# Odd steps of a state-space scan: rows brought by a repeating DMA and copied to PSUM by ScalarE instead of a spreading matmul

## The reference, cut to what matters

```python
xr, gate = jnp.split(x @ W_in.T, 2, axis=-1)
...
xc = silu(conv(xr))                        # 4 taps, over tokens
xn = (xc - mu) / jnp.sqrt(var + 1e-05) * ln_g + ln_b
Bm, Cm, dt = jnp.split(xn @ W_xproj.T, 3, axis=-1)
...
def step(h, inputs):
    ad, bd, xt, ct = inputs
    h = jnp.clip(h * ad[:, :, None] + bd[:, :, None] * xt[:, None, :], -10.0, 10.0)
    yt = jnp.einsum('bd,bdh->bh', ct, h)
    return (h, yt)
_, ys = jax.lax.scan(step, h0, ...)        # 1024 steps, one behind the other
y = ys + D * xn
return y * jax.nn.silu(gate) @ W_out.T
```

## Time and profile before

| what | value |
|---|---|
| median of 3 runs | 6216.15 us (6211.86 to 6225.62) |
| profiled execution, own time | 6190.74 us |
| its span | 6188.9 us |
| mean granted PE clock | 0.972 of full speed |
| attention phase | 0 to about 3142 us |
| first to last step of the scan | 3323 to 6097 us |
| the tail behind it | 6097 to 6189 us |

### The profile page before, as it was taken

The page is one execution under the profiler, slowest core; times in us unless marked ns, Lnnn a source line. Parts: engine busy times, 40 slices in busy tenths (PEclk is TensorE's granted clock), DMA queues, the critical chain, the costliest instruction groups (busy, mean ns, idle before and its releaser), DMA issues. The chain is left out here.

```text
span 6188.9 us, 73250 instructions
## 1 busy us (share of the span) xinstructions
PE 5830.7 (94%) x24000; PEld 2703.2 (44%) x24000; DVE 4474.3 (72%) x5676; ACT 2407.5 (39%) x4698; POOL 3217.6 (52%) x2625
## 2 busy tenths in 40 slices
PE   7999999999999999999986879999999999999998
PEld 3444444444444444444443424444443444444343
DVE  4656656556556566565546998999999898999983
ACT  2444444445444454444453424243332423334111
POOL 1876767677667776775743323425243443524213
PEclk7999999999999999999988889999999999999999
DMA  2332323333232332323213343534444443544433
GB/s 86 89 91 69 99 73 94 91 88 89 76 96 77 98 93 69 106 60 96 82 67 109 87 113 103 147 96 131 110 116 126 121 133 89 150 96 128 115 91 115
DMA packets 411565, 613.30 MB, mean 99 GB/s; under 512 B 58768, under 2 KB 189968, under 8 KB 410672
## 3 DMA queue, kind: packets, MB, share of 16 engines
q1 hardware_dynamic: 374320, 558.24, 32.4%
q10 hardware_dynamic: 36864, 50.38, 3.2%
HBM read 305.31 MB, written 201.38 MB: 82 GB/s over the span
## 5 line engine op out<-in xcount | busy, mean ns | idle before, releaser
L1126 POOL TENSOR_TENSOR acc<-acc,prob 128x512 f32<-128x512 f32 x1536 | 1906.4, 1277 | 837.3 <-PE bank L815 570.8
L1055 DVE TENSOR_REDUCE mx<-bank 128x1 f32<-128x512 f32 x2048 | 1307.4, 684 | 535.9 <-PE bank L785 529.6
L2091 DVE SCALAR_TENSOR_TENSOR g<-xps,bd,g 128x1024 f32<-128x1024 f32 x1024 | 1313.2, 1282 | 143.8 <-PE xps L1806 68.1
L1806 PE MATMUL xps<-sx,spread 128*128 128x512 f32 x2048 | 910.4, 529 | 140.6 <-DVE g L2091 126.0
L948 ACT ACTIVATE prob<-misc 128x512 f32<-128x512 f32 x1277 | 713.5, 599 | 739.0 <-PE misc L802 653.6
L785 PE MATMUL bank<-khat,qhat 96*128 96x512 f32 x2048 | 939.1, 519 | 5.9 <-DVE mx L1055 0.9
L2097 DVE TENSOR_SCALAR g<-g,lim 128x1024 f32<-128x1024 f32 x1024 | 892.7, 872 | 34.8
L1806 PEld LDWEIGHTS xps<-sx,spread 128*128 128x128 f32 x2048 | 359.0, 195 | 693.8 <-issue 368.0
L802 PE MATMUL misc<-qhat,khat 98*128 98x512 f32 x1443 | 602.6, 460 | 17.8 <-ACT prob L948 11.7
L785 PEld LDWEIGHTS bank<-khat,qhat 96*128 96x128 f32 x2048 | 373.8, 192 | 532.5 <-issue 381.4
L1820 PE MATMUL yps<-g,cexp 128*32 128x512 f32 x4096 | 585.4, 630 | 0.1
(11 more groups left out here) (221 smaller groups left out, 7189.6 us busy)
## 6 DMA issues: line engine op xcount, KB each, us to landing
sx<-scratch_xhl SPq DMA_DIRECT2D x512, 128.0 KB, 4.9
scratch_dx<-dx SPq DMA_DIRECT2D x64, 512.0 KB, 3.2
scratch_xhl<-xhi SPq DMA_DIRECT2D x64, 512.0 KB, 4.9
scratch_xhl<-xn SPq DMA_DIRECT2D x64, 512.0 KB, 5.1
scratch_y<-ysb SPq DMA_DIRECT2D x512, 64.0 KB
dx_t<-scratch_dx SPq DMA_DIRECT2D x59, 512.0 KB, 6.1
y_t<-scratch_y SPq DMA_DIRECT2D x59, 512.0 KB, 3.9
xt_n<-in_x SPq DMA_DIRECT2D x112, 256.0 KB, 3.0
```

Source lines behind the costliest of these rows:

```text
L1055: dve.tensor_reduce(self.mx2[:, h * TT + qt, c:c + 1], bank[m][:, 0:QC], AX.X, ALU.max).then_inc(sem[f"dve_m{m}"], 1)
L1126: pool.tensor_tensor(self.acc[:, a, h, :], self.acc[:, a, h, :], self.prob[:, (n % 2) * GH + h, :], ALU.add).then_inc(sem["pool_acc"], 1)
L1806: mm = pe.matmul(self.xps[t % 2][:, half * BANK:(half + 1) * BANK], self.spread[:, 2 * part + half, :], self.sx[:, n % 2, wd, :], start=Tr ...
L2091: dve.scalar_tensor_tensor(self.g[:, t % 4, :], self.xps[t % 2][:, :], self.bd[:, i % 2, tl:tl + 1], self.g[:, (t - 1) % 4, :], ALU.mult, ...
```

## The change

Even steps are as before. For odd steps:

- the normalised rows of odd tokens are stored from `xn` to a new DRAM tensor `scratch_xrow` after `a2` (`sxr`, two semaphores, 64 partitions of a tile each time); `lo` waits for that store, since it overwrites `xn`. The stores `shi` and `slo` take even tokens only, and `scratch_xhl` is half as large.
- SP loads one row of all 8 batches per odd step, each batch repeated 16 times by a step of zero in the source, into a ring of four buffers of 128 x 1024 in SBUF (`lr`, 512 KB on the SBUF side).
- ACT copies the buffer into the PSUM pair (`xa`), waiting for `q` of step `t - 2` and for the load. A buffer is loaded again when its copy is done, for the step 8 later.
- the matmul pair of odd steps goes, and a unit's four `sx` loads are half as large.
- `q` waits for `g(t-1)` first, then for the copy or the matmul; `x` waits for `q(t-2)` first.
- for room in SBUF, `y_t` and `dx_t` share their memory with constants that are used before them, and the constants' loads of the scan share one semaphore, for which each engine waits when it comes to the scan.

The core of the diff (left out: the merged waits on `ld_const` in the other places):

```diff
@@ -1130,6 +1130,7 @@
 
+ROWS = 4
 LAST_ROOMS = 3
...
@@ -1267,11 +1268,12 @@
                         put("POOL", 1.27, ("a2", i, hb, bb, half), (("a1", i, hb, bb, half),), [("pool_x", 1)], port=True)
+                    put("SP", 0.55, ("sxr", i, hb, bb), (("a2", i, hb, bb, 1),) + ((("sxr", i, hb, bb - 2),) if bb > 1 else was("sxr", *old, HB - 2 + bb)), [(f"st_xr{bb % 2}", 16)], lands=4.0)
                     for half in range(2):
...
                     for half in range(2):
-                        put("POOL", 1.27, ("lo", i, hb, bb, half), (("hi", i, hb, bb), ("sq", i, hb, bb), ("a3", i, hb, bb, half)),
+                        put("POOL", 1.27, ("lo", i, hb, bb, half), (("hi", i, hb, bb), ("sq", i, hb, bb), ("a3", i, hb, bb, half), ("sxr", i, hb, bb)),
                             [("pool_lo", 1)], port=True)
...
@@ -1376,19 +1378,32 @@
             put(n * UNIT - 12.0, "SP", 2.2, ("lu", n), (rows if n * UNIT % TOK == 0 else ()) + (
-                (("x", (n - 1) * UNIT - 1),) if n > 1 else (("rest",),)), [(f"ld_sx{n % 2}", 64)], lands=4.0)
+                (("x", (n - 1) * UNIT - 2),) if n > 1 else (("rest",),)), [(f"ld_sx{n % 2}", 64)], lands=4.0)
+
+        def row(t):
+            i = t // TOK
+            put(t - 7.0, "SP", 0.6, ("lr", t), tuple(("sxr", i, hb, bb) for hb in range(2) for bb in range(HB)) + (
+                (("xa", t - 2 * ROWS),) if t > 2 * ROWS else ()), [(f"ld_xb{t // 2 % ROWS}", 16)], lands=4.0)
 
...
             put(t - 2.0, "PE", 0.45, ("x", t), (("lu", t // UNIT),) + ((("q", t - 2),) if t > 1 else ()), [("pe_xps", 1)])
+
+        def copy_of(t):
+            put(t - 2.0, "ACT", 1.05, ("xa", t), (("lr", t),) + ((("q", t - 2),) if t > 1 else ()), [("act_xps", 1)])
+
         for n in range(2):
             load(n)
-        x_of(0), x_of(1)
+        for t in range(1, 2 * ROWS, 2):
+            row(t)
+        x_of(0), copy_of(1), row(1 + 2 * ROWS)
         for t in range(last):
             i, tl = divmod(t, TOK)
-            put(t, "DVE", 1.3, ("q", t), (("x", t),) + ((("g", t - 1),) if t else (("g0",),)) + ((("d3", i),) if tl == 0 else ()) + (
+            put(t, "DVE", 1.3, ("q", t), (("xa", t) if t % 2 else ("x", t),) + ((("g", t - 1),) if t else (("g0",),)) + ((("d3", i),) if tl == 0 else ()) + (
                 (("out", (t - 4) // 2 * 2),) if t > 3 else ()), [("dve_q", 1)], step=t)
             if t + 2 < last:
-                x_of(t + 2)
+                (copy_of if t % 2 else x_of)(t + 2)
+            if t % 2 and t + 2 + 2 * ROWS < last:
+                row(t + 2 + 2 * ROWS)
             put(t, "DVE", 0.82, ("g", t), (("q", t),), [("dve_g", 1)], port=True)
...
@@ -1449,7 +1464,9 @@
         self.wx = sb("wx", [P, CT, NX])
-        self.wxdt = sb("wxdt", [NST, DIN])
+        early = sb("early", [P, 2 * DIN])
+        y_t, dx_t = early[:, 0:DIN], early[:, DIN:2 * DIN]
+        self.wxdt = early[0:NST, 0:DIN]
         self.wdt = sb("wdt", [NST, NST])
...
@@ -1457,9 +1474,9 @@
         self.mask = sb("mask", [P, 8, 32])
-        self.ones_at = sb("ones_at", [P, 4 * P])
-        self.tmp = sb("tmp", [P, CT, NX])
-        self.ones = sb("ones", [P, P])
+        self.ones_at = early[:, DIN:DIN + 4 * P]
+        self.tmp = early[:, DIN + 4 * P:DIN + 4 * P + CT * NX].rearrange("p (t k) -> p t k", t=CT)
+        self.ones = early[:, DIN + 4 * P + CT * NX:DIN + 5 * P + CT * NX]
         self.gw = sb("gw", [P, NX])
...
@@ -1490,13 +1507,12 @@
 
-        self.sx = sb("sx", [P, 2, UNIT // 2, BANK], F32R)
+        self.sx = sb("sx", [P, 2, UNIT // 4, BANK], F32R)
+        self.xb = sb("xb", [P, ROWS, DIN])
 
...
         self.ysb = sb("ysb", [P, 2, BANK])
-        y_t = sb("y_t", [P, DIN])
-        dx_t = sb("dx_t", [P, DIN])
         sg = sb("sg", [P, DIN])
...
@@ -1598,23 +1614,39 @@
                 w.wait_ge(sem["act_hi"], plan.after("act_hi", ("hi", i, hb, bb)))
-                sp.dma_start(d["xhl"][0, hb * HB + bb, i * TOK:(i + 1) * TOK, :].bitcast(F32),
-                             self.xhi[:, bb % 2, :].bitcast(F32)).then_inc(sem[f"st_xhi{bb % 2}"], 16)
+                sp.dma_start(d["xhl"][0, hb * HB + bb, i * TOK // 2:(i + 1) * TOK // 2, :].bitcast(F32),
+                             self.xhi[0:P:2, bb % 2, :].bitcast(F32)).then_inc(sem[f"st_xhi{bb % 2}"], 16)
             elif kind == "slo":
...
                 w.wait_ge(sem["pool_lo"], plan.after("pool_lo", ("lo", i, hb, bb, 1)))
-                sp.dma_start(d["xhl"][1, hb * HB + bb, i * TOK:(i + 1) * TOK, :].bitcast(F32), self.xn[:, bb, :]).then_inc(
-                    sem[f"st_xlo{bb}"], 16)
+                sp.dma_start(d["xhl"][1, hb * HB + bb, i * TOK // 2:(i + 1) * TOK // 2, :].bitcast(F32),
+                             self.xn[0:P:2, bb, :]).then_inc(sem[f"st_xlo{bb}"], 16)
+            elif kind == "sxr":
+                i, hb, bb = at
+                w.wait_ge(sem["pool_x"], plan.after("pool_x", ("a2", i, hb, bb, 1)))
+                w.wait_ge(sem.get(f"st_xr{bb % 2}"), plan.before(f"st_xr{bb % 2}", p))
+                sp.dma_start(d["xrow"][hb * HB + bb, i * TOK // 2:(i + 1) * TOK // 2, :], self.xn[1:P:2, bb, :]).then_inc(
+                    sem[f"st_xr{bb % 2}"], 16)
+            elif kind == "lr":
+                t, = at
+                i, k = t // TOK, t // 2 % ROWS
+                for hb in range(2):
+                    for bb in range(HB):
+                        w.wait_ge(sem[f"st_xr{bb % 2}"], plan.after(f"st_xr{bb % 2}", ("sxr", i, hb, bb)))
+                if t > 2 * ROWS:
+                    w.wait_ge(sem["act_xps"], plan.after("act_xps", ("xa", t - 2 * ROWS)))
+                sp.dma_start(self.xb[:, k, :], d["xrow"][:, t // 2, :].unsqueeze(1).broadcast_to([B, NST, DIN])).then_inc(
+                    sem[f"ld_xb{k}"], 16)
             elif kind == "lu":
                 n, = at
-                i, s, t0, wd = n * UNIT // TOK, n % 2, n * UNIT, UNIT // 2
+                i, s, t0, wd = n * UNIT // TOK, n % 2, n * UNIT // 2, UNIT // 4
 
...
                 if n > 1:
-                    w.wait_ge(sem["pe_xps"], plan.after("pe_xps", ("x", (n - 1) * UNIT - 1)))
+                    w.wait_ge(sem["pe_xps"], plan.after("pe_xps", ("x", (n - 1) * UNIT - 2)))
                 else:
...
@@ -1796,11 +1828,11 @@
                 n, r = divmod(t, UNIT)
-                part, wd = divmod(r, UNIT // 2)
+                part, wd = divmod(r // 2, UNIT // 4)
+                if t > 1:
+                    w.wait_ge(sem["dve_q"], plan.after("dve_q", ("q", t - 2)))
                 w.wait_ge(sem["dve_set"], plan.after("dve_set", ("rest",)))
                 w.wait_ge(sem[f"ld_sx{n % 2}"], plan.after(f"ld_sx{n % 2}", ("lu", n)))
-                if t > 1:
-                    w.wait_ge(sem["dve_q"], plan.after("dve_q", ("q", t - 2)))
                 for half in range(2):
...
@@ -1992,6 +2023,13 @@
                                bias=self.state_cols[:, 0:1]).then_inc(sem[f"act_m{m}"], 1)
+            elif kind == "xa":
+                t, = at
+                k = t // 2 % ROWS
+                if t > 1:
+                    w.wait_ge(sem["dve_q"], plan.after("dve_q", ("q", t - 2)))
+                w.wait_ge(sem[f"ld_xb{k}"], plan.after(f"ld_xb{k}", ("lr", t)))
+                act.activation(self.xps[t % 2][:, :], self.xb[:, k, :], ACT.Copy).then_inc(sem["act_xps"], 1)
             elif kind == "ysb":
...
@@ -2081,11 +2118,14 @@
                 i, tl = divmod(t, TOK)
-                w.wait_ge(sem["dve_set"], plan.after("dve_set", ("g0",)))
-                w.wait_ge(sem["pe_xps"], plan.after("pe_xps", ("x", t)))
-                w.wait_ge(sem["dve_par"], plan.after("dve_par", ("d3", i)))
                 if t:
                     w.wait_ge(sem["dve_g"], plan.after("dve_g", ("g", t - 1)))
+                if t % 2:
+                    w.wait_ge(sem["act_xps"], plan.after("act_xps", ("xa", t)))
+                else:
+                    w.wait_ge(sem["pe_xps"], plan.after("pe_xps", ("x", t)))
+                w.wait_ge(sem["dve_set"], plan.after("dve_set", ("g0",)))
+                w.wait_ge(sem["dve_par"], plan.after("dve_par", ("d3", i)))
                 if t > 3:
...
@@ -2366,7 +2407,7 @@
     for name, shape, dt in (("rows", (B, 3, HID), F32), ("xs", (B, S, HID), F32), ("x2", (B, S, HID), F32), ("x2T", (HID, B, S), F32),
-                            ("dx", (B, S, DIN), F32), ("xhl", (2, B, S, DIN), F32R),
+                            ("dx", (B, S, DIN), F32), ("xhl", (2, B, S // 2, DIN), F32R), ("xrow", (B, S // 2, DIN), F32),
                             ("y", (B, S, DIN), F32)):
```

More of the change, by code:

```diff
@@ L1523, in __init__ @@
         self.sem = self.plan.sems
-        for name in ("win", "const", "late", "wx", "cols", "sc", "spread", "wxdt"):
+        for name in ("win", "const", "late"):
             name = f"ld_{name}"
@@ L1569, in sync @@
         sp.dma_start(self.mask[:, :, :], d["mask"].rearrange("p (a m) -> p a m", a=8)).then_inc(sem["ld_const"], 16)
```

(24 more changed lines are left out.)

## The result

The changed kernel takes 6456.0 us (6451.5 to 6459.3), the one before 6214.0 us beside it: a ratio of 1.039 (1.037 to 1.041), so it is 3.9% slower.

What follows compares the result with a forecast made beforehand. DVE and PE bound the scan before; eight full DMA engines would after. Middle, first and last parts add 250, 10 and 45 us, +305 on 6216: 6521 us. Own range 6380 to 6660; 8-in-10 range 6070 to 6900.

Steps and rivals of the forecast that it cites:

- Part 5: DMA engines in the scan: row loads fill eight of sixteen, 13.8 us each per unit, becoming the new bound: +305 us.
- the prediction's own test: Lone row loads: the prediction is wrong if they show share 1.0 instead of 0.5, or 0.5 lasting under 2.8 us.
- the prediction's terms: Busiest engines' other work per middle unit: 7.14 us each after removals, plus scratch_y stores, 11.5 engine-us over four engines.
- Part 1: PE in the scan: 512 matmul pairs go, 341 us less PE work in the middle; 101 us of DVE's waits won.
- I count 75: DVE's waits for PE: 75 us counted as won in the middle scan, plus 26 in the last, together 101.
- Part 2: Wait order of `q` in the scan: asking for `g(t-1)` first saves 0.037 us per step, 34 us taken.
- Part 3: 512 ACT copies from SBUF to PSUM at odd steps: 1.05 us each, costing nothing on the path.
- Part 4: SP issues 512 row loads and 64 stores, about 0.4 us each; POOL's wait and the constants' semaphore are also covered.
- Rival A: Row loads run on all sixteen engines, DVE is the bound and 135 us are won: 6081 us; chance 0.21.
- B: Row loads on eight engines at the clean store rate, 22 engine-us per row: about 6185 us; chance 0.12.
- C: Row loads on eight engines with interfering writes, at `khat`'s rate: 4.15 us per row, 27.7 per middle unit; chance 0.21.
- D: ACT's copy late or SP held: 0.3 us at every second odd step, 77 us; chance 0.06.

Runs made afterwards that it cites:

- the spread stores: Changed kernel with scratch_y laid out so its stores have 32 outermost entries and use sixteen DMA engines, row loads unchanged: 6350.4 us, 1.025 of the kernel before.
- sixteen engines: Changed kernel with each odd row stored twice in DRAM, so row loads have sixteen outermost entries, each repeated eight times: 6183.0 us, 0.9979 of the kernel before.
- 16-channel run: Changed kernel whose row loads bring only 16 of 1024 channels, all issues and copies kept: 6123.1 us, 0.989 of the kernel before.
- the ACT queue: Changed kernel with row loads issued by ACT on its own DMA queue instead of SP's: 6648.1 us, 1.073 of the kernel before.
- the half version: Changed kernel where, at odd steps, PE builds channels 0 to 511; a sixteen-engine row load and ACT bring the rest: 6211.7 us, 1.003 of the kernel before.

## Why the prediction was right, and where it was not

Forecast 6521 us, 305 more; measured 6456, 242 more (261 in the profiled spans), inside the forecast's own range of 6380 to 6660.

Part 5, the bound, held, and so did its count: the row loads on eight engines are what costs. The lone row load shows 0.48 where the prediction's own test asked for 0.5. Its price, in engine-us (microseconds of one DMA engine), from a 6 us window around one:

```profile
3525.00:3531.00 6.00, 3.17 (x14) 1.08 (x14) 5.86 (x6) 2.49 (x5) 3.48 (x3) 1.00 0.31 94
```

0.31 x 6 x 16 = 29.8 engine-us, 3.7 us on each of eight; 3.44 was taken from the `affine` load of the earlier trace rows. In bulk: 0.62 x 24.3 x 16 = 241 per unit, less the other work by the prediction's terms, 16 x 7.14 + 11.5 = 126, leaves 28.9 per row, 3.6 us on each engine. By this sum the four busiest carry 10.0 + 4 x 3.6 = 24.4 us of a unit of 2334 / 96 = 24.3, and the other four of the eight 21.5.

So the row was a little too cheap (13.8 for 14.4 us per unit). But the sum now asks for engines without a gap, and the trace has gaps. The longest, in the middle part:

```profile
3944.10:3950.60 6.50, 6.25 (x40) 4.06 (x39) 5.45 (x9) 1.90 (x3) 2.84 (x3) 1.00 0.00 0
```

By the packet records no packet is in flight for 87 of the 2334 us, so no engine can be busy for more than 96%, which is the filling that the prediction took from PE. (It is PE's in the middle part; in the last one has 98%.) Fewer than eight packets are in flight for 21% of the time, so the eight are never all busy for more than 79%. For 10% of the time there are more than sixteen: packet times then overlap on an engine, and engine-us add up to more than busy time. The prices of the sum are therefore too high where the load is heavy, and the 24.8 forecast for 24.3 owes something to errors that cancel. The engines are the bound in the sense that unloading them gives the time back, not in the sense that they are full. That late loads delay the copies, and so the next row loads, would explain the gaps; it was not followed up. By stage: +250, +10 and +45 us forecast, +206, +16 and +37 measured. That the four engines of `scratch_y` are among the eight was an assumption; the 106 us of the spread stores speak for it, and nothing in the traces shows engine numbers. The rule of the Trainium skill that the prediction weighed ("DMA: Bandwidth & Descriptors", "Why a DMA increments its semaphore by 16 and not by 1"), the largest k up to 16 that divides the slowest dimension, fits all three cases: 0.48 with eight entries, 0.26 with four, and with sixteen a share of 0.72, which alone says only more than eight, with sixteen packets in flight.

What failed is where the wait would show. The prediction had ACT's copies and `q` at odd steps wait for the ring. They did so for 9.0 and 15.8 us. (The landing time of the row loads, which it wanted far above 5 us, no view of after gives; with sixteen engines it is 6.1.) It had costed only the row load's own consumer, and passed over the other loads in the same engines: `x2T_t` has one buffer and no lead, so it is the first to suffer, and PE's written order carries the delay to the even steps. The total came out near all the same because it was added up from the load of the engines, and not from who waits; that the two errors of that sum point in opposite directions helped. PE's busy share was forecast at 75% and is 85%: busy time does not fall with the number of matmuls. 769 fewer in the middle part took away 45 us, not 341 (103 us in the 16-channel run, where the granted clock is as before). `xps` halved (682.5 to 341.9 us), while other groups became longer. `yps` rose from 429.7 to 484.9, though one of its matmuls takes 613 ns where it took 620, and to 506.0 in the 16-channel run, so the clock is not the reason there: spans of matmuls overlap, and a group's busy time holds what no neighbour covers. The matmuls that wait for `x2T_t` did take longer each, 681 for 603 ns (372.0 to 423.3 us), at a granted clock of 0.93 instead of 0.99.

Part 1 was sized too high, which no one sees in after, but the 16-channel run does: parts 1 and 2 without the bytes are worth 70 us, not 135. By stage 3, 41 and 28 us; the last part was right (31 forecast), the middle was not (about 100). The row behind it:

```profile
DVE proj L2201 <- PE miscb L1814: 39.8, 14, 5.6
```

`proj` waited 52.9 us before. Only 13 go. What is late there is probably a chain through PE and ACT (PE's matmuls before `proj` wait for ACT in all these runs) and not the mass of PE's work; no run tests it. DVE's busy time rose by 13 us as well (1949 to 1963). The step "I count 75" took waits for PE to be waits for PE's load.

Part 2's mechanism and size held: 0.07 us per step above the clip's, gone with the order. What arrives depends on what is behind it: 14 us of 38 in the kernel before, and in after 11, which is not clear of noise. Part 3 held: a copy takes 1.025 us (1.05 taken), and costs the path 15.8 us. Part 4 held in its verdict, though a row's issue takes 0.6 us, not 0.4: the 16-channel run has all of the issues, POOL's wait and the constants, and is faster than before.

Rival A had the right picture of sixteen engines and the wrong price: 10 us under before, not 135. Of the 125 us between, 65 are the gain of parts 1 and 2 that was not there, and 60 separate this run from the one with 16 channels: its mean share is 0.73, not 0.33, `x2T_t` lands at 4.6 us instead of 3.1, and PE waits 49 us for the two loads instead of 11. B falls by the price of a row, 29 and not 22 engine-us. C's rate is that of the load's start: the 2 us shown move 123 GB/s, 15.4 per engine, where `khat` has 15.8, but the 2 us that begin 1.2 us later move 176, 22 per engine:

```profile
3528.00:3530.00 2.00, 1.13 (x8) 0.17 (x6) 1.93 (x3) 0.89 (x1) 1.17 (x1) 1.00 0.45 176
```

By the packet records the load's 128 packets take 28.5 engine-us. The median is 0.159 us, which for all of them would be 20.4, as the store of `scratch_dx` has it; 6.6 of the 8.1 above that belong to packets that start in the first microsecond. So a row is 3.6 to 3.7 us of each engine, not 4.15, and a unit took 24.3 us, not 27.7. D did not occur.

Still open: why the first packets of a row load take longer than those of a store of the same size, how much of the loss is the engines' time and how much the loads that come too late for PE, whether other loads than x2T matter, and the two surprises above (the ACT queue and the half version).

## What to carry to other kernels

Count a new transfer's time on the engines that it really uses, not in the mean share: its outermost dimension says how many those are, and at a mean DMA share of 0.62 they were the bound here. Splitting the outermost dimension into sixteen, even at the cost of storing the data twice, gave back 273 us. When engines are heavily loaded, look for the transfer with the least lead, not for the one added; and before taking work from an engine at 96%, look at how much of the other's waiting is that engine's load, for that alone can be won.

## What the runs showed of the hardware

An instruction with two waits started 0.091 to 0.104 us behind its predecessor when the wait that ended last was written second, and 0.035 or 0.036 us when it was written first (the most frequent gaps between `g` and `q`, with the old order and the new). With row loads on eight engines, and the kernel held up by them, the mean share was 0.62, no packet was in flight for 3.7% of the time and fewer than eight for 21%. A lone row load moved 123 GB/s over its start and 176 later. The latency of a 256 KB load grew from 3.1 us at a share of 0.33 to 3.7 and 4.6 at 0.52 (eight engines busier than the rest) and 0.73 (even), and to 7.5 us at 0.62, with whole row loads on eight engines. ACT's copy of 128x1024 from SBUF to PSUM took 1.025 us, against 1.049 from SBUF to SBUF.
